# A two-layer graph kernel whose adjacency matrix is laid out chunk by chunk

## What is computed

```python
h = maximum(layernorm(x), 0)
Wh = h @ W0;  e = leaky_relu((Wh @ a[:128])[:, None] + (Wh @ a[128:])[None, :], 0.2)
alpha = softmax(where((adj > 0) | eye, e, -9e15), axis=1)
x = x + alpha @ Wh
h = maximum(layernorm(x), 0)
weights = where(adj < 1.0, exp(-(1/adj - 1)**2 / 0.5), 0.0)
x = x + weights @ (h @ W1 + B1)
```

## Time and profile before

| | us |
|---|---|
| median of 3 runs | 217.57 (216.57 to 217.8) |
| the profiled execution | 217.44 |
| its span, first to last instruction | 215.6 |

### The profile page before, as it was taken

The page is one execution under the profiler, slowest core; times in us unless marked ns, Lnnn a source line. Parts: engine busy times, 40 slices in busy tenths (PEclk is TensorE's granted clock), DMA queues, the critical chain, the costliest instruction groups (busy, mean ns, idle before and its releaser), DMA issues.

```text
span 215.6 us, 3229 instructions
## 1 busy us (share of the span) xinstructions
PE 154.3 (72%) x956; PEld 103.7 (48%) x970; DVE 182.0 (84%) x535; ACT 189.3 (88%) x207; POOL 132.8 (62%) x140
## 2 busy tenths in 40 slices
PE   0186779983794992989929997499392977799472
PEld 0074565440362760549615844186341654668361
DVE  7993999999979999999488796995986499878855
ACT  0699987599899999999999999799999994999960
POOL 3980002295000588888878888888787788667450
PEclk9999999996599698599985999999979799999995
DMA  5999999999999999999999999999999999961303
GB/s 166 355 413 410 410 408 408 409 411 405 418 418 409 409 393 405 391 400 393 402 388 387 394 401 394 404 387 400 394 387 389 386 401 393 406 229 43 115 23 103
DMA packets 22259, 76.81 MB, mean 356 GB/s; under 512 B 2527, under 2 KB 3126, under 8 KB 22240
## 3 DMA queue, kind: packets, MB, share of 16 engines
q1 hardware_dynamic: 18912, 71.31, 84.7%
q0 software_dynamic: 2912, 5.22, 7.0%
q10 hardware_dynamic: 416, 0.07, 0.2%
HBM read 74.06 MB, written 4.23 MB: 363 GB/s over the span
## 4 chain that ended last, share of the span: by engine, by line
DMA 36%; DVE 31%; PE 18%; issue 7%; ACT 5%; SPq 1%; POOL 1%; POOLq 0%; DVEq 0%
DMA adj_ring<-in_adj 35%; DVE summed L1134 10%; PE bank L642 9%; DVE cand L1172 3%; ACT spread L921 3%; DVE hub_w L1415 3%; PE bank L769 2%; DVE x_sb L1458 2%; PE bank L754 2%; PE bank L761 2%; SPq L383 1%; DMA gathered_rows<-node_table,shared_index 1%; DVE stats L1114 1%; PE bank L629 1%; DVE shared_slots L1230 1%
## 5 line engine op out<-in xcount | busy, mean ns | idle before, releaser
L544 POOL DMA_INDIRECT gathered_rows<-node_table,index x48 | 76.0, 1584 | 36.5 <-DVE index L1309 22.5
L952 ACT ACTIVATE trash_a<-adj_ring,below_one 128x4096 fp8e4<-128x4096 f32 x19 | 70.4, 3705 | 5.7 <-DMA adj_ring<-in_adj 5.2
L642 PE MATMUL bank<-adj_ring,pack_w 128*128 128x512 bf16 (+3 forms) x255 | 70.0, 402 | 2.4 <-DMA adj_ring<-in_adj 1.5
L961 ACT ACTIVATE trash_a<-adj_ring 128x4096 fp8e4<-128x4096 f32 x19 | 68.7, 3614 | 0.5
L1134 DVE SCALAR_TENSOR_TENSOR summed<-adj_ring 128x4096 fp8e4<-128x4096 f32 x13 | 58.0, 4458 | 4.3 <-DMA adj_ring<-in_adj 4.2
L642 PEld LDWEIGHTS bank<-adj_ring,pack_w 128*128 128x128 bf16 x262 | 26.1, 104 | 31.5 <-issue 8.8
L544 POOL DMA_INDIRECT gathered_rows<-node_table,shared_index x24 | 33.2, 1382 | 9.6 <-issue 6.7
L1172 DVE MAX8 cand<-bank 128x8 f32<-128x120 f32 (+25 forms) x82 | 23.3, 351 | 3.9 <-PE bank L642 3.9
L769 PE MATMUL bank<-gathered_rows,spread 128*128 128x129 f32 x160 | 20.9, 282 | 3.9 <-DVE spread L1398 2.4
L769 PEld LDWEIGHTS bank<-gathered_rows,spread 128*128 128x128 f32 x160 | 19.4, 194 | 5.1 <-issue 4.8
L629 PE MATMUL bank<-codes,code_w 128*128 128x512 bf16 x25 | 11.2, 448 | 8.5 <-DMA adj_ring<-in_adj 5.6
(11 more groups left out here) (190 smaller groups left out, 258.4 us busy)
## 6 DMA issues: line engine op xcount, KB each, us to landing
adj_ring<-in_adj SPq DMA_DIRECT2D x32, 2048.0 KB, 23.6
node_table<-gathered_rows POOLq DMA_DIRECT2D x4, 520.0 KB, 8.3
x_sb<-in_x SPq DMA_DIRECT2D x8, 256.0 KB, 5.9
out<-x_sb SPq DMA_DIRECT2D x3, 512.0 KB, 14.2
gathered_rows<-node_table,index POOLq DMA_INDIRECT x48, 5.9
gathered_rows<-node_table,shared_index POOLq DMA_INDIRECT x24, 5.4
out<-x_sb SPq DMA_DIRECT2D x2, 192.0 KB, 2.1
out<-x_sb SPq DMA_DIRECT2D x1, 128.0 KB, 1.9
```

Source lines behind the costliest of these rows:

```text
L544: pool.indirect_dma_start(out=rows[:, g % RING_GROUPS * GE + t, :], out_offset=None, in_=table, in_offset=bass.IndirectOffsetOnAxis(ap=row ...
L642: last = nc.tensor.matmul(to[:, lo:hi], pack_w[:, k, :], ring_hi[:, i % AR, row_at + lo:row_at + hi], start=False, stop=(k == KB - 1), ski ...
L952: nc.scalar.activation(trash_a[:, :], ring[:, i % AR, :], ACT.Sign, bias=below_one[:, :], scale=-1.0, accum_out=signs[:, n:n + 1], saturat ...
L961: nc.scalar.activation(trash_a[:, :], ring[:, i % AR, :], ACT.Abs, accum_out=sizes[:, n:n + 1], saturate=False).then_inc(checked_a, 1)
```

## The change

On the host, before the launch, the kernel function copies `adj` into a second array, `adj_laid`, in which the 32 chunks follow one another in the order of loading, each as 128 partitions of 16 KB. The array is one more input in HBM; the program gets `adj` as well, for its general path. `load_chunk` reads chunk i as one block, a partition's 16 KB in one piece. Nothing else differs.

```diff
-    adj_chunks = adj.rearrange("(s h k p) (c n) -> s c h p k n", s=SG, h=2, k=HK, p=P, n=CW)
...
             def load_chunk(i):
-                s, c, h = chunk(i)
-                sp.dma_start(ring[:, i % AR, :].rearrange("p (k n) -> p k n", k=HK),
-                             adj_chunks[s, c, h]).then_inc(adj_ready[i % AR], 16)
+                sp.dma_start(ring[:, i % AR, :], adj_laid[i]).then_inc(adj_ready[i % AR], 16)
...
+def chunks_laid_out(adj, np):
+    laid = np.empty((CHUNKS, P, HK * CW), adj.dtype)
+    for i in range(CHUNKS):
+        s, c, h = chunk(i)
+        planes = adj[s * HR + h * HK * P:s * HR + (h + 1) * HK * P, c * CW:(c + 1) * CW].reshape(HK, P, CW)
+        laid[i] = planes.transpose(1, 0, 2).reshape(P, HK * CW)
+    return laid
...
+    laid = chunks_laid_out(arrays["in_adj"], np)
+    arrays["adj_laid"] = laid
+    args.append(nc.dram_tensor("adj_laid", laid.shape, mybir.dt.from_np(laid.dtype), kind="ExternalInput").ap())
```

More of the change, by code:

```diff
@@ L145, with gnn_program @@
 ADD_OWN_AT = {13: 0, 21: 1, 29: 2}
-def gnn_program(nc, x, adj, w0, a0, w1, b1, out):
+def gnn_program(nc, x, adj, w0, a0, w1, b1, adj_laid, out):
     fp32, bf16, fp8, i32, u32 = (mybir.dt.float32, mybir.dt.bfloat16, mybir.dt.float8e4, mybir.dt.int32,
```

## The result

The changed kernel takes 221.24 us (median of 4, 220.68 to 221.97), the kernel before beside it on the same chip 217.07 us (median of 4): a ratio of 1.019, 95% interval 1.014 to 1.024. It is slower, by 4.2 us.

The account below looks back on a forecast made before the run. Transport and engines were taken as close to even, with POOL's gather chain beside them. Faster loads remove DVE's load waits, but late table and gathers add 1.0 us: 217.44 + 1.0 = 218.4 us, range 213.6 to 224.

Parts of the forecast that it names:

- its own case: Whole kernel: waits for loads are replaced by waits for gathers, 218.4 us, from 216 to 220.5; chance 42%.
- the second rival: Gathers between issue and landing are held far longer, up to 9.3 us more: 227 us, half of it 222.7; chance 22%.
- Transport: Load queue: 768 fewer descriptor starts on each DMA engine save 7 us, last load lands at 185.5.
- Turns: DMA engines: queues alternate one descriptor each, so another queue's turn beside a load costs 0.616 us instead of 0.161.
- The table: POOL's table stores: 38 turns cost 14.5 us, landing at 77.1 instead of 62.6, first gather near 78.0.
- A gather beside loads: POOL's gathers of table rows: data and semaphore turns make each land 0.7 us later.
- First and fourth group: DVE's waits for gather groups: first late by 4 to 5 us, fourth a new wait of 3.5 us.
- the chain is four gathers back: POOL's gather chain: the first gather, held by DVE's check until 82.4, puts the chain 5.4 us back, not 6.3.
- Seventh group: DVE's wait for the seventh group of gathers: landed at 177.8 instead of 171.7, DVE 1.0 us later than before.
- DVE works without a gap that matters: From the seventh group to the end: no further wait on DVE, so its 1.0 us goes to the end.
- not held up: Gathers beside 16 KB descriptors: other queues get in between, only transport changes, 214.7 us; chance 25%.
- cut into 4 KB: Loads in the DMA engines: split into 4 KB anyway, nothing changes, 217.4 us; chance 11%.

Follow-up runs that it names:

- 16 KB for 6 to 11: Changed kernel with 16 KB load descriptors only for chunks 6 to 11, 4 KB for all others: 219.98 us, ratio 1.016 to the kernel before.
- 4 KB for 6 to 9: Changed kernel with 4 KB load descriptors for chunks 6 to 9, 16 KB for all others: 215.41 us over ten executions, ratio 0.991 to the kernel before.
- the run with 38 repeats: Changed kernel with TensorE issuing chunk 28's first code matmul 38 times instead of once: 219.88 us, against 221.30 for the changed kernel beside it.

## Why the prediction was right, and where it was not

The mechanism was the one forecast, the loss was larger: 221.2 where it said 218.4. That is inside the whole range, but above the 216 to 220.5 that the forecast gave its own case; it was covered by the room left above for the second rival at half price (222.7), which is not what happened. So far the number was right by luck. By its steps:

- *Transport.* 768 starts on each engine at 9 ns made 7 us and a last load at 185.5; it landed at 185.0, 7.5 us earlier than before, or 9.8 ns a start. (The forecast's own line leaves 9.7 ns, 0.163 less 4 x 0.0383 us; the 9 was cut short.) The Trainium skill (DMA: Bandwidth & Descriptors, section Why small descriptors are slow) gives some 3 cycles, by which an estimate was 2.7 us; the trace does not agree.
- *Turns.* One to one, with a load descriptor of 0.616 us forecast and measured: 92 packets beside 90 between 57 and 61 us, 473 beside 471 between 54 and 74. Equal counts alone do not tell one at a time from several at a time; the gathers do, which land 0.4 to 0.9 us later, where waiting behind several load descriptors of 0.616 us would take longer. The same page of the Trainium skill (section Queues, rings and completion order) has an engine change queues only between packets, a packet being typically 9 to 17 descriptors. The first agrees with these rows, the second does not for the loads. And what the prediction calls a descriptor is a packet, which on POOL's queue can hold several rows: the 2,912 packets are 608 for the table and the hub's rows and 32 for each of 72 gathers, 16 of them semaphore writes, so a gather's 128 rows travel in 16.
- *The table.* Forecast to land at 77.1, landed at 76.9; the 38 turns, semaphores counted, were sized well, with a little luck. The last store was issued 0.9 us later than before, which the forecast did not have; from its issue to its landing took 24.5 us instead of 11.1, so the turns were worth 13.4 us and not 14.5. The kernel with 16 KB for 6 to 11 has the same 24.5. The first gather started at 77.86 for 78.0 and was held until 83.1 for 82.4.
- *A gather beside loads.* 0.7 us later forecast, 0.4 to 0.9 measured at 16 KB and 0.1 to 0.3 at 8 KB (medians of the profiles). This throws out the upper bound of 9.3 us and with it the second rival.
- *First and fourth group.* 4 to 5 us forecast for the first, 4.88 measured. 3.5 us for the fourth, 5.33 measured: the step "the chain is four gathers back" was mis-sized. The fourth group's last gather started at 138.18, 7.9 us later than in the earlier trace rows and not 5.4. From the first gather to that one, five issues fell beside a check of DVE and took 4 to 5 us, before only four. Which ones are caught depends on how the two rows of work happen to lie, and a chain that is moved by 5 us meets other checks.
- *Seventh group.* Forecast to land at 177.8 and to make DVE 1.0 us late; it landed at 179.2 and made DVE 2.5 us late. Its last gather started only 4.0 us later than before, at 170.05, but within DVE's check of 168.76, took 4.03 us to issue instead of 1.0, and landed 9.1 us after its start. The forecast moved the gathers and DVE's checks each by their own terms, and did not look which gather would then lie beside which check. The profile with 4 KB for 6 to 9, where that gather started 1.2 us earlier and was not caught, shows what this is worth.
- *From there to the end.* "DVE works without a gap that matters" failed. PE, idle for 8.1 us because DVE was, came back at a lower clock, and DVE waited 1.43 us for it; the run with 38 repeats shows this term as 1.1 to 1.4 us. With the 1.5 us of the seventh group it makes up what the forecast lacked: 218.4 + 1.5 + 1.4 = 221.3.

Of the rivals, "not held up" fell with the table's landing and "cut into 4 KB" with 6,624 packets on q1. What none of them had was the way in which a wait of DVE for a gather comes back through TensorE's clock.

Open is why POOL's wait ahead of its first pass is longer in kernels that begin with 16 KB loads, and whether that is the whole of their spread: a long or late pass was seen in five of their eight profiles, and the other executions have none.

## What to carry to other kernels

Before the descriptors of a large stream are made bigger, count the turns that small, urgent transfers take beside it, semaphore writes included, and multiply them by the time of the new descriptor: here 8 KB gave 5.3 of the 7.5 us of transport and left the table in time, and 16 KB made it late. Small descriptors only for the loads under way in the urgent stretch did as well in most executions, but not in those in which the urgent transfer itself came later than that stretch. When a chain is moved, look anew at which of its steps lie beside work that holds them; here a gather caught or missed by a check was worth 3 us. And price a new wait by what stands idle with it: 8 us of waiting on TensorE cost some 1.1 to 1.4 us more at the clock it came back with.

## What the chip showed that was not expected

- A semaphore write beside 16 KB loads waits a whole turn: four more on each engine moved the table by 2.4 us, and 485 packets of q0, semaphore writes among them, went beside 483 of q1. The Trainium skill (DMA: Bandwidth & Descriptors, section Anatomy of one DMA — SWDGE (gpsimd) path) calls the write essentially free; that can hold for the write itself, but not for its place in the queue, by these rows.
- TensorE's granted clock fell to 0.78 over the stretch behind 2.5 us without work in one kernel and stayed at 1.00 behind 1.5 us in another; behind 8.1 us it was 0.53 to 0.62.
- A POOL pass of 1.92 us took 6.1 to 6.2 us when it began between 43.29 and 43.39, at or just behind the start of DVE's check. Begun at 43.00, it kept its 1.92 us, and the check took 5.9 us instead of 4.4; begun at 47.89, behind the check, it took 1.92 us again.
